# Recommender tower kernel: gathered rows on partition 32*quad + field, half tile's products as groups of 64 rows, layer 2's first product as four column groups

## The reference

```
e = stack([tbl_f[ids[:, f]] for f in 32 fields])            # x: (1024, 32, 32)
h = x
for W, b in ((W0, b0), (W1, b1), (W2, b2)):                 # 128, 128 and 1 outputs
    z = relu(einsum('bhd,bmd,ohm->bod', h, x, W) + b)       # all pairs (h row, x row), per embedding column d
    h, direct = z[:, :64], z[:, 64:]                        # last layer: direct = z
z = sum over d of the direct parts                          # (1024, 129)
y = relu(relu([z, dense_ctx] @ W_top1 + b1) @ W_top2 + b2) @ W_top3
```

## Time and profile before

| | |
|---|---|
| median of 3 runs | 1159.18 us (1158.91 to 1159.81) |
| profiled execution | 1164.29 us, span of the records 1162.5 us |
| PE busy | 1116.8 us (96% of the span) |
| DVE busy | 1083.0 us (93%) |
| ACT busy | 458.8 us (39%) |
| POOL busy | 520.5 us (45%) |
| PE weight loads | 652.8 us (56%), beside the products |
| mean granted TensorE clock | 0.994 |

### The profile page before, as it was taken

The page is one execution under the profiler, slowest core; times in us unless marked ns, Lnnn a source line. Parts: engine busy times, 40 slices in busy tenths (PEclk is TensorE's granted clock), DMA queues, the critical chain, the costliest instruction groups (busy, mean ns, idle before and its releaser), DMA issues.

```text
span 1162.5 us, 10957 instructions
## 1 busy us (share of the span) xinstructions
PE 1116.8 (96%) x3608; PEld 652.8 (56%) x3608; DVE 1083.0 (93%) x604; ACT 458.8 (39%) x383; POOL 520.5 (45%) x270
## 2 busy tenths in 40 slices
PE   0699999999999999999999999999999999999998
PEld 0355555556555555556555565555555555555554
DVE  1599999999999999999999999999999999999963
ACT  0134444333444433344444334444333444443424
POOL 6702445654445555454456544455555544450000
PEclk9899999999999999999999999999999999999999
DMA  7654543466554435555543455454445545433200
GB/s 222 200 165 129 148 136 118 108 153 162 161 139 137 126 108 143 161 161 139 132 135 106 140 161 161 139 146 128 112 129 160 161 140 160 131 123 96 55 1 0
DMA packets 63413, 154.94 MB, mean 133 GB/s; under 512 B 12753, under 2 KB 29394, under 8 KB 63394
## 3 DMA queue, kind: packets, MB, share of 16 engines
q1 hardware_dynamic: 52562, 146.98, 42.5%
q0 software_dynamic: 8192, 4.21, 3.0%
q10 hardware_dynamic: 2640, 3.50, 1.0%
HBM read 95.79 MB, written 8.39 MB: 90 GB/s over the span
## 4 chain that ended last, share of the span: by engine, by line
PE 93%; issue 2%; DVE 2%; ACTq 1%; another core or an unknown queue 1%; ACT 1%; DMA 0%; SPq 0%; DVEq 0%
PE z_ps L543 89%; PE u_ps L543 2%; PE mlp_ps L543 1%; DVE raw L450 1%; DVE prod_lo L457 1%; DVE prod L411 1%; DMA h_roll<-h_roll 0%; SPq L328 0%; ACT prod_hi L760 0%; SPq L329 0%; ACT h_roll L729 0%; ACT direct L747 0%; ACTq L713 0%; ACTq L715 0%
## 5 line engine op out<-in xcount | busy, mean ns | idle before, releaser
L543 PE MATMUL z_ps<-prod,w_sb 128*128 128x512 f32 x1536 | 692.8, 597 | 39.2 <-issue 28.4
L303 POOL DMA_INDIRECT gathered<-in_table,rows_sb x256 | 504.9, 1972 | 499.5 <-DVE h2x L464 428.8
L543 PEld LDWEIGHTS z_ps<-prod,w_sb 128*128 128x128 f32 x1536 | 292.7, 191 | 350.6 <-issue 333.8
L760 ACT CAST prod_hi<-raw 128x2048 fp32r<-128x2048 f32 x128 | 243.9, 1905 | 396.5 <-DVE raw L450 389.4
L450 DVE TENSOR_TENSOR raw<-h_roll,x_roll 128x2048 f32<-128x2048 f32 x128 | 293.1, 2290 | 5.6 <-DMA h_roll<-h_roll 2.1
L457 DVE TENSOR_TENSOR prod_lo<-raw,prod_hi 128x2048 fp32r<-128x2048 f32 x128 | 292.0, 2281 | 2.6 <-ACT prod_hi L760 2.6
L411 DVE TENSOR_TENSOR prod<-h_roll,x_roll 128x2048 f32<-128x2048 f32 x128 | 292.6, 2286 | 0.0
L543 PE MATMUL z_ps<-prod_hi,w_hi 128*128 128x512 f32 x520 | 215.4, 494 | 0.4 <-DVE prod_lo L457 0.4
L543 PE MATMUL z_ps<-prod_lo,w_hi 128*128 128x512 f32 x520 | 164.1, 395 | 0.0
L543 PE MATMUL z_ps<-prod_hi,w_lo 128*128 128x512 f32 x520 | 163.8, 395 | 0.0
L411 DVE TENSOR_TENSOR prod<-x_base,x_roll 128x2048 f32<-128x2048 f32 x63 | 143.4, 2286 | 12.8 <-DMA x_roll<-x_dram 10.8
(11 more groups left out here) (56 smaller groups left out, 240.8 us busy)
## 6 DMA issues: line engine op xcount, KB each, us to landing
x_roll<-x_dram SPq DMA_DIRECT2D x128, 512.0 KB
x_base<-x_dram SPq DMA_DIRECT2D x32, 512.0 KB
h_roll<-h_roll SPq DMA_DIRECT2D x32, 448.0 KB, 4.6
h_roll<-h_roll SPq DMA_DIRECT2D x32, 384.0 KB, 5.4
h_roll<-h_roll SPq DMA_DIRECT2D x32, 320.0 KB
x_dram<-gathered SPq DMA_DIRECT2D x64, 128.0 KB
h_roll<-h_roll SPq DMA_DIRECT2D x32, 192.0 KB
gathered<-in_table,rows_sb POOLq DMA_INDIRECT x256
```

Source lines behind the costliest of these rows:

```text
L303: nc.gpsimd.indirect_dma_start(gathered[:, u, g * DIM:(g + 1) * DIM], None, table, bass.IndirectOffsetOnAxis(ap=rows_sb[:, col:col + 1], a ...
L543: return nc.tensor.matmul(*args, **kw)
L760: nc.scalar.copy(prod_hi[:, b % SPLIT_RING, :, :], raw[:, :, :]).then_inc(hi_ready, 1)
```

## The change

Gathered rows go to partition 32*quad + field instead of 4*field + quad. With that the 64 partitions 0 to 63 hold quads 0 and 1, and 64 to 127 hold quads 2 and 3. The half tile's product for a quad then takes only those 64 rows as its contraction, with two weight tiles instead of four (rows of the half's other quad are zero), ordered so that the two halves alternate. Layer 2's first product becomes four products with 32 weight columns each, one for every group of 32 output partitions. The DRAM side of the two stores and of `x_part16` takes the quad as its outermost dimension. Weight layouts, the ids and the placement of the rounding rest (four transfers of 16 partitions instead of one of 64) follow.

```diff
-        w16_sb = sb("w16_sb", [P, QUADS, P], F32R)
+        w16_sb = sb("w16_sb", [P, PAIR, P], F32R)
-        w2_sb = sb("w2_sb", [P, 2, P])
+        w2_sb = sb("w2_sb", [P, PAIR, FIELDS])
...
                 for copy in range(2):
                     to = bass.AP(x_dram.tensor, at + copy * (FIELDS * CHUNK),
-                                 [[CHUNK, FIELDS], [PART, QUADS], [1, PART]])
+                                 [[PART, QUADS], [CHUNK, FIELDS], [1, PART]])
                     sp.dma_start(to, gathered[:, u, :]).then_inc(x_stored[u % 2], 16)
...
                 sp.dma_start(x_part16[:, s, :], bass.AP(x_dram.tensor, at + FIELDS // 2 * CHUNK,
-                                                        [[CHUNK, FIELDS], [PART, QUADS], [1, PART]])
+                                                        [[PART, QUADS], [CHUNK, FIELDS], [1, PART]])
                              ).then_inc(x_part16_loaded[s], 16)
...
             def layer0_pairs16(c):
                 pe.wait_ge(lo16_ready, c + 1)
-                for q in range(QUADS):
-                    cols = slice(q * PART, (q + 1) * PART)
-                    mm(z0_ps[:, cols], w16_sb[:, q, :], hi16[:, :], start=False, stop=False)
-                    last = mm(z0_ps[:, cols], w16_sb[:, q, :], lo16[:, :], start=False,
-                              stop=(q + 1) * PART % BANK == 0)
+                for t in range(PAIR):
+                    for part in (hi16, lo16):
+                        for half in range(PAIR):
+                            q = PAIR * half + t
+                            rows = slice(half * HID, (half + 1) * HID)
+                            last = mm(z0_ps[:, q * PART:(q + 1) * PART], w16_sb[rows, t, :], part[rows, :],
+                                      start=False, stop=t == PAIR - 1 and part is lo16)
                 last.then_inc(pairs16_used, 1)
...
-                for t in range(2):
-                    last = mm(u_ps[:, :], w2_sb[:, t, :], h2[:, u % 2, t * PART:(t + 1) * PART],
-                              start=t == 0, stop=t == 1)
+                for q in range(QUADS):
+                    half, t = divmod(q, PAIR)
+                    last = mm(u_ps[FIELDS * q:FIELDS * (q + 1), :], w2_sb[:, half, :],
+                              h2[:, u % 2, t * PART:(t + 1) * PART], start=True, stop=True)
...
-            act.dma_start(w16_raw[P // 2:P, :, :], w16_rest[P // 2:P, :, :]).then_inc(w16_rest_placed, 16)
+            for q in range(QUADS):
+                low_half = slice(FIELDS * q + FIELDS // 2, FIELDS * (q + 1))
+                act.dma_start(w16_raw[low_half, :, :], w16_rest[low_half, :, :]).then_inc(w16_rest_placed, 16)
```

More of the change, by code:

```diff
@@ L163, in build_tower @@
         early = h_roll[:, 1, 0:3, :].rearrange("p a (t n) -> p (a t) n", n=P)
-        w0_swap, w16_raw, w16_swap, w16_rest = [early[:, 4 * k:4 * (k + 1), :] for k in range(4)]
+        w0_swap = early[:, 0:ROLLS, :]
+        w16_raw, w16_swap, w16_rest = [early[:, ROLLS * k:ROLLS * k + PAIR, :] for k in range(1, 4)]
         w1_raw = early[:, 16:24, :]
@@ L376, in _ @@
             sp.wait_ge(eye_stored, 16)
-            sp.dma_start(quad_ones[:, :], bass.AP(eye_dram.tensor, 0, [[0, FIELDS], [FIELDS, QUADS], [1, FIELDS]])
+            sp.dma_start(quad_ones[:, :], bass.AP(eye_dram.tensor, 0, [[FIELDS, QUADS], [0, FIELDS], [1, FIELDS]])
                          ).then_inc(ones_ready, 16)
@@ L506, in step @@
                         sum_z2(group - 1)
-            dve.wait_ge(w16_rest_placed, 16)
+            dve.wait_ge(w16_rest_placed, 16 * QUADS)
             nc.vector.tensor_copy(w16_sb[:, :, :], w16_raw).then_inc(w16_ready, 1)
@@ L845, in lay_out @@
     arrays = {"table": np.concatenate(tables, axis=0)}
-    arrays["gather_ids"] = a["ids"].reshape(UNROLL, QUADS, CHUNKS // UNROLL, GATHERS, FIELDS).transpose(4, 1, 2, 0, 3).reshape(P, -1)
-    arrays["row_base"] = np.repeat(first_row[i][:, None], UNROLL * GATHERS, axis=1)
+    arrays["gather_ids"] = a["ids"].reshape(UNROLL, QUADS, CHUNKS // UNROLL, GATHERS, FIELDS).transpose(1, 4, 2, 0, 3).reshape(P, -1)
+    arrays["row_base"] = np.repeat(first_row[r % FIELDS][:, None], UNROLL * GATHERS, axis=1)
     w0 = a["L0_rec_W0"].reshape(P, FIELDS, FIELDS)
-    w0_tiles = np.zeros((P, ROLLS + QUADS, P), w0.dtype)
+    w0_tiles = np.zeros((P, ROLLS + PAIR, P), w0.dtype)
     w0_swapped = np.zeros_like(w0_tiles)
@@ L859, in lay_out @@
     for q in range(QUADS):
-        for rows in (QUADS * low + q, QUADS * (low + FIELDS // 2) + q):
-            w0_tiles[rows, ROLLS + q, :] = w0[:, low, low + FIELDS // 2].T
-            w0_swapped[rows, ROLLS + q, :] = w0[:, low + FIELDS // 2, low].T
+        for rows in (FIELDS * q + low, FIELDS * q + low + FIELDS // 2):
+            w0_tiles[rows, ROLLS + q % PAIR, :] = w0[:, low, low + FIELDS // 2].T
+            w0_swapped[rows, ROLLS + q % PAIR, :] = w0[:, low + FIELDS // 2, low].T
     arrays["w0"], arrays["w0_swapped"] = w0_tiles, w0_swapped
@@ L869, in lay_out @@
     w2 = a["L0_rec_W2"].reshape(HID, FIELDS)
[L870 to L873, removed]
+    w2_tiles = np.zeros((P, PAIR, FIELDS), w2.dtype)
+    for half in range(PAIR):
+        w2_tiles[half * HID:(half + 1) * HID, half, :] = w2
     arrays["w2"] = w2_tiles
```

## The result

The changed kernel takes 1179.28 us (median of 4 runs, 1177.3 to 1180.32) against 1159.05 us: ratio 1.0171, 95% interval 1.0154 to 1.0189. That is 20 us slower, and outside the forecast range. The profiled execution is 15.1 us longer than the profiled one of before (spans 1177.6 and 1162.5 us).

A forecast was written before the change was run, and what follows sets the result against it. PE and DVE were both taken as at the limit, DVE through its x_roll[3] loop. 2.0 - 0.5 + 1.4 - 2.2 - 0.1 = +0.6 on the profiled 1164.29 gives 1164.9, unprofiled 1159.8 us; range 1155.5 to 1166.

The forecast's parts named there:

- The bound: PE and DVE both at their limit; PE alone getting faster buys at most the distance by which it trails DVE.
- PE's section: Half tile and u on PE: 1.41 us a chunk instead of 1.81, 0.40 less, hidden by DVE's loop.
- the rival with serial products: 64-row products on PE don't overlap: section 1.88 us, 0.07 more, about 1163 us; chance 15%.
- End and tail: After the gathers stop, PE takes b3's last pairs at once, -2.2 us; the last u after the loop, -0.1.
- Stores on four engines: The stores' packets go over four engines, 3.2 us, so x_base is issued 2.0 us later.
- Start: First load without cover: +2.0 us for the later x_base, -0.5 for the first half tile.
- The middle: Later x_base mostly covered before x1: 0.05 us a chunk over 28 chunks, +1.4 us; bounds 0 and 10 us.
- the late burst is not covered: x_roll[3] or x_part16 lands late in most chunks: 1164 us at 0.2 a chunk, 1168 at 0.35; chance 20%.
- My two chunks of the earlier trace: Two chunks with x_base 1.7 us late: 0.35 us extra wait before x1 in one, none in the other.
- `x_part16` hidden: x_part16 on four engines takes 1.2 us more, just hidden before raw16 reads it: 0 us.

The follow-up runs named there:

- e1_flat: The changed kernel with the DRAM side of the two stores and of x_part16 described as before the change: 1158.30 us, ratio 0.9978.
- e5_flat_reorder: e1_flat with x_part16 issued ahead of x_roll[3] and DVE making raw16 between x0 and x1: 1150.27 us, ratio 0.9887.
- e6_before_reorder: The kernel before with only x_part16 issued ahead of x_roll[3] and raw16 made between x0 and x1: 1160.22 us, ratio 0.9985.
- e9_one_narrow: The changed kernel with the second of the two stores written field outermost on the DRAM side, the first as changed: 1162.15 us, ratio 1.0005.
- e3_part_narrow: The changed kernel with the two stores' DRAM side as before the change, x_part16 left as changed: 1157.63 us, ratio 0.9977.
- the reorder: SP issues x_part16 ahead of x_roll[3] and DVE makes raw16 between x0 and x1; alone on the kernel before: 1160.22 us, ratio 0.9985.
- e8_split: The changed kernel with each store cut by quad, the second copy only its 16 read fields and issued from ACT: 1160.61 us, ratio 0.9987.

## Why the prediction was wrong

I forecast no change at 1159.8 us; it is 1179.3. Point by point:

*The bound: right.* Both engines at the limit, DVE's through the loop over x_roll[3], and PE's gain hidden by it: `e1_flat` keeps the pace at 33.77. I had worked out that DVE without its wait needs 33.43 us a chunk; `e5_flat_reorder`, without it, takes 33.43. That they agree to 0.01 is luck: the 0.37 was one chunk's idle time, and the mean before x1 over the chunks from the third on is 0.23.

*PE's section: right, the saving a little small.* I had 0.40 us less a chunk; start to start it is 0.49. The halves overlap, so the rival with serial products is out. It has no part in the loss.

*End and tail: right.* -2.2 and -0.1 forecast, -2.5 and +0.2 measured. PE took b3's pair of chunk 30 4.5 us after DVE had begun it; now it is 2.6:

```profile
1106.74 2.29 DVE L412 TENSOR_TENSOR prod<-h_roll,x_roll 128x2048 f32<-128x2048 f32 x1
1109.35 3.59 PE L544 MATMUL z_ps<-prod,w_sb 128*128 128x512 f32 x8
```

*Stores on four engines: right in kind, delay 3.0 instead of 2.0 us.* Their movement takes 3.60 - 1.15 = 2.45 us longer, for which 12.7/4 gave 2.0; the packets are slower on four engines (3.6 x 4/256 = 0.056 us each instead of 0.050). The first begins to move 1.3 us after the issue instead of 0.8 (717.30 - 716.04 against 567.50 - 566.72), and SP's issues themselves are longer (1.47 against 0.86). The Trainium skill, page "DMA: Bandwidth & Descriptors", section "Why a DMA increments its semaphore by 16 and not by 1", gives the largest number up to 16 that divides both sides' slowest dimension, here 4. The share of 0.25 agrees.

*Start: +1.5 forecast (2.0 - 0.5), +2.7 measured to the first direct sum.* The first product came at 29.65 where 27.07 was, 2.6 us later for 2.0 forecast. But layer 0's activations are at 41.69, 2.1 us earlier than before. The first half tile can't have given that back: it takes 1.5 us in the kernel before and 0.7 now. In the kernel before the activation starts 5.2 us after the last half tile record has ended, with nothing in the trace that says why, and now 0.04 us after; in the trace of `e6_before_reorder`, with the same half tile, it is 0.03. So the earlier trace rows's 43.78 was a late one, and this part of the comparison is worth little. What is late for a reason is the second chunk, of which I had not spoken. Its `x_base` comes 8.4 us after its store, since the store's few engines still have the first chunk's loads to do (timeline of SP, then DVE; before, x1 of this chunk was made at 43.40):

```profile
29.90 1.22 SPq L322 DMA_DIRECT2D x_dram<-gathered  x2
38.28 0.60 SPq L347 DMA_DIRECT2D x_base<-x_dram  x1
```

```profile
50.88 2.29 DVE L412 TENSOR_TENSOR prod<-x_base,x_roll 128x2048 f32<-128x2048 f32 x1 [1.99 <-DMA x_roll<-x_dram]
```

That those loads are in the way is read from the times and was not tried. The first sum of the five kernels with flat stores and no pause lies at 93.05 (`e1_flat`) to 98.65 and is 96.1 in the mean; of the four with narrow ones it lies at 99.21 to 103.77, 101.5 in the mean. So the start costs nearer 5 us than 2.7, an estimate from single executions, and the kernel before with its 98.23 was one of the late ones. In unprofiled runs the loss is 20.2 us instead of 15.1; the difference is the 5.1 us by which before's profiled execution was long. The late start is about half of that; the rest I can't place.

*The middle: the step that failed.* "I take 0.05 a chunk, since one of two shows nothing and a plain delay leaves the loop's own issue untouched: +1.4". It is 0.51 a chunk, +14.7, beyond my upper bound of 0.35. The mechanism is the rival "the late burst is not covered", which I had priced at 1164 to 1168 and given 20%. Two errors are in that sentence. The bounds came from chunks with a delay of 1.7 us, and the cost is no line through them: 1.6 us is nearly free (`e9_one_narrow`), 3.0 costs 20 us, so bounds read at 1.7 say nothing of 3.0 (nor of the 2.0 that I had forecast). And that the issue of x_roll[3] is untouched was true and no protection: a transfer issued in time behind others that are not yet moved lands late. The landings tell what I should have looked for: in the kernel before the last packet of x_roll[2] lands 1.1 us ahead of x_roll[3]'s issue (mean over the chunks from the third on), in the changed kernel 2.1 us behind it; and x_roll[3] itself, whose loop sets DVE's pace, lands 4.81 us after its issue instead of 4.28, which is the 0.5 us a chunk. The mean is made by few chunks: in the seven that wait over 1 us x_roll[2] ends 3.7 to 5.6 us behind that issue and x_roll[3] takes 5.3 to 6.9 us; in all others x_roll[2] ends at most 3.8 us behind it and x_roll[3] takes at most 5.3. My two chunks of the earlier trace rows were at 2.7 and 3.2 us, both just short of where it begins to cost. In my experiments' expectations I put the cover at 1.1 us, the mean distance; that was too simple, since an overlap of up to 3.3 us is harmless and what costs is how many chunks go beyond it.

*`x_part16` hidden: right* (`e3_part_narrow`).

## What to carry to other kernels

When a transfer gets another slowest dimension, count the engines that will move it, and look at who waits for its last packet: here SP does, and everything behind it in SP's queue came late. A cover measured at one delay says nothing about twice that delay; find out chunk by chunk how far the burst behind it already reaches into the transfer that sets the pace, and how far it may (here 3.3 us), and price the chunks that a longer delay pushes beyond that, at the full rate of the loop. And when two bounds lie within a per cent of each other, test each edit with the other bound lifted: alone PE's edit and the reorder were worth 0.2% each, neither clear of no change, together 1.1%.

## What was not expected of the hardware

- A pair of stores of 256 rows of 1 KB takes 3.60 us on four engines and 1.15 us on sixteen, and `x_base` behind it is 3.0 us later, more than the 2.0 us that the old time per packet on four engines gives.
- Cut by quad (32 partitions to a transfer, half of the second copy left out), the stores no longer hold the burst up for long, but eight issues instead of two still leave `x_base` 1.1 us later (`e8_split`).
- A transfer that is issued on time behind one still in flight is hardly late while that one ends within 3.3 us of the issue (its reader waits 0.9 us at most); where that one ends 4 us or more after it, the reader waits 1.2 to 3.8 us (300 chunks of ten kernels).
- A row of 512 bytes to DRAM and the wait for it is a pause of only 1.1 us.
- Products with 64 rows on the two halves of the array, in float32r, run side by side with their weight loads: the two of a pair start 0.004 us apart, the pairs 0.12 us, so eight take the time of four.
